# Causal attention beside an FP4 gated layer: one stream over the batches, the layer's products cut up between the score halves

## What is computed

```python
qkv = x @ Wqkv.T                                   # 16 heads of 16 channels
dots = jnp.einsum('bhid,bhjd->bhij', q, k) * scale
dots = jnp.where(causal_mask, -jnp.inf, dots)
attn = jax.nn.softmax(dots, axis=-1)
out = jnp.einsum('bhij,bhjd->bhid', attn, v)
...                                                # heads side by side
return out @ Wout.T + bout

gate = fp4_linear(x, w_gate)                       # 256 -> 704; x and the weights rounded
y = fp4_linear(x, w_up)                            # to FP4 in blocks of 16
h = jax.nn.silu(gate) * y
return fp4_linear(h, w_down)                       # 704 -> 256
```

## Time and profile before

| | us |
|---|---|
| median of 3 runs | 2636.86 (2636.82 to 2639.11) |
| span of the profiled execution | 2634.3 |
| of it from the first scores of `main_phase` on | 1646 |
| TensorE, ScalarE, VectorE busy in the whole span | 2291.5, 1991.2, 1901.9 |

### The profile page before, as it was taken

How to read it: one execution, slowest core, us unless ns; L and a number is a source line. 1 busy time by engine, 2 the same in 40 slices (tenths; PEclk the granted TensorE clock), 3 DMA queues, 4 the chain that set the end, 5 groups by cost and what they waited for, 6 DMA issues and landing times.

```text
span 2634.3 us, 89616 instructions
## 1 busy us (share of the span) xinstructions
PE 2291.5 (87%) x34104; PEld 1276.1 (48%) x34104; DVE 1901.9 (72%) x5676; ACT 1991.2 (76%) x3470; POOL 645.3 (24%) x524
## 2 busy tenths in 40 slices
PE   2896999999999957888888888888888888888888
PEld 1784444444444424444445444545454445444455
DVE  6675999999999965656656666665676565566565
ACT  1343999999999957888875888885888884887885
POOL 3212233333333321212211222211122211222211
PEclk9897999999999989999999999999999999999999
DMA  2576445555555522011012011021111021110101
GB/s 61 177 227 143 69 73 72 73 73 72 73 73 72 73 36 64 21 22 30 23 47 62 18 27 30 16 57 50 24 31 30 15 60 45 27 30 16 27 18 34
DMA packets 94822, 144.19 MB, mean 55 GB/s; under 512 B 25264, under 2 KB 74160, under 8 KB 93872
## 3 DMA queue, kind: packets, MB, share of 16 engines
q1 hardware_dynamic: 73456, 113.77, 23.1%
q10 hardware_dynamic: 16576, 15.73, 1.9%
q0 software_dynamic: 4352, 8.92, 1.4%
HBM read 104.20 MB, written 34.14 MB: 53 GB/s over the span
## 4 chain that ended last, share of the span: by engine, by line
PE 31%; ACT 12%; issue 11%; DVE 7%; ACTq 1%; DMA 0%; SPq 0%; POOL 0%; DVEq 0%; POOLq 0%
ACT probs L1129 10%; PE O L998 8%; PE F L1019 8%; PE F L1059 6%; PE S L977 5%; PE S L1070 2%; PE F L1049 1%; DVE h_norm L1282 1%; DVE o_turned L1344 1%; DVE o_turned L1345 1%; ACT ht_hi L1144 1%; DVE fp_step L1280 1%; DVE fp_step L1278 1%; PE F L1012 1%; PE S L983 0%
## 5 line engine op out<-in xcount | busy, mean ns | idle before, releaser
L1129 ACT ACTIVATE probs<-S 128x1024 f32<-128x1024 f32 (+3 forms) x1280 | 1056.0, 907 | 143.6 <-issue 52.8
L775 ACT ACTIVATE m_excess<-m_DIFF 128x512 f32<-128x512 f32 (+7 forms) x1536 | 646.9, 472 | 85.7 <-PE m_DIFF L735 39.9
L793 DVE CUSTOM_DVE_ANT_0 m_excess<-m_S,m_excess 128x512 f32<-128x512 f32 (+7 forms) x1536 | 700.6, 530 | 11.8 <-PE m_S L735 9.5
L998 PE MATMUL O<-probs,v_sb 64*32 64x512 f32 (+3 forms) x10240 | 611.3, 534 | 33.3 <-DVE o_turned L1345 29.3
L977 PE MATMUL S<-q_st,k_st 64*32 64x512 f16 (+3 forms) x10240 | 432.2, 353 | 180.6 <-ACT probs L1129 140.9
L733 PE MATMUL m_S<-m_k,m_q 128*128 128x512 f16 (+7 forms) x1536 | 482.9, 325 | 26.7 <-DVE m_row_max L793 17.3
L733 PE MATMUL m_DIFF<-m_k,m_q_diff 128*128 128x512 f16 (+7 forms) x1536 | 477.7, 319 | 26.5 <-DMA m_q_diff<-s_q 26.2
L977 PEld LDWEIGHTS S<-q_st,k_st 64*32 64x32 f16 x10240 | 136.1, 90 | 588.7 <-ACT probs L1129 480.4
L677 POOL TENSOR_TENSOR m_q_diff<-m_zero,m_q 48x4096 f16<-48x4096 f16 x32 | 224.4, 7012 | 428.9 <-DMA m_q<-s_q 418.2
L733 PEld LDWEIGHTS m_S<-m_k,m_q 128*128 128x128 f16 x1536 | 148.3, 97 | 275.8 <-DVE m_row_max L793 195.1
L1307 DVE TENSOR_SCALAR tanh<-tanh 128x352 int32<-128x352 int32 x128 | 49.4, 386 | 273.9 <-ACT decay L1139 273.9
(11 more groups left out here) (178 smaller groups left out, 3923.0 us busy)
## 6 DMA issues: line engine op xcount, KB each, us to landing
m_q<-s_q SPq DMA_DIRECT2D x96, 128.0 KB, 3.8
m_k<-s_k SPq DMA_DIRECT2D x96, 128.0 KB, 6.7
m_q_diff<-s_q SPq DMA_DIRECT2D x96, 128.0 KB, 8.0
k_st<-s_k SPq DMA_DIRECT2D x96, 128.0 KB, 4.3
q_st<-s_q SPq DMA_DIRECT2D x384, 32.0 KB
m_k<-s_k SPq DMA_DIRECT2D x96, 124.0 KB, 5.3
a_x<-in_L_attn_x_dram POOLq DMA_DIRECT2D x16, 512.0 KB, 4.8
s_q<-a_part SPq DMA_DIRECT2D x32, 256.0 KB, 2.5
```

Source lines behind the costliest of these rows:

```text
L775: act.activation(excess[u % MAX_EXCESS][:, 0:keys // 2], DIFF[u % MAX_BUFS][:, 0:keys // 2], ACT.Relu) \
L793: dve.tensor_tensor_reduce(larger, S[u % MAX_BUFS][:, 0:keys // 2], larger, 1.0, -3e38, ALU.add, ALU.max, column).then_inc(reduced[u % MAX ...
L998: ins = pe.matmul(O[e][s * SLOT:(s + 1) * SLOT, st.skip:QC], v_sb[st.hg % 2][rows, st.j, s * SLOT:(s + 1) * SLOT], probs[s // 2][st.n % PR ...
L1129: act.activation(probs[half][st.n % PROBS][:, :, 0:st.width], S[half][:, :, 0:st.width], ACT.Exp, scale=scale).then_inc(exped[half], 1)
```

## The change

The four batches become one list of 640 steps, unrolled, with constants in all waits and no loop. The layer's 64 tiles run on through the batches. Each tile has 20 marks, spread evenly over the 10 steps by `place_marks`, which counts a step as its queries plus 110; a mark that falls into the first half of a step is in `early`, the others in `late`. Each engine does its pieces of a mark at the place of `early` or `late` in its own program. On TensorE `early` stands between the two score halves and `late` after the second, ahead of the values. The gate's and the up product are cut into halves of three matmuls, `down` into five pieces of three or four, `h_turn` into two (four and two transposes). The output projection of a batch is made two tiles at a time in `F[0]` and `F[1]` while the next batch's attention runs (from the last three tiles of a batch on, 8 tiles long); only the last ten of the 64 stay for the end. x tiles go into a ring of three of their own, and SyncE issues their loads and the stores. The queries of a chunk are now loaded a chunk ahead. Cut to its core:

```diff
-X_TURN_AT, PAIR_AT, FIRST_PAIR_AT = 2, {4: 0, 7: 1}, {5: 0, 8: 1}
-H_TURN_AT, DOWN_AT = 0, 2
-LAST_H_TURN_AT = 9
+def place_marks(steps, b):
+
+    ends, total = [], 0
+    for st in steps:
+        total += st.width + STEP_COST
+        ends.append(total)
+    at = 0
+    for n in range(TILES):
+        for k in range(MARKS):
+            due = (n * MARKS + k + 0.5) * total / (TILES * MARKS)
+            while ends[at] <= due:
+                at += 1
+            half = ends[at] - (steps[at].width + STEP_COST) / 2
+            (steps[at].early if due < half else steps[at].late).append((b * TILES + n, k))
+
+
+X_TURN_AT = 4
+GATE_AT, UP_AT = ((7, 8), (11, 12)), ((9, 10), (13, 14))
+H_TURN_AT = (16, 17)
+DOWN_AT = (19, 0, 1, 2, 3)
+X_HIGH_AT, GATE_PARTS_AT, H_HIGH_AT = 4, (8, 12), (16, 17)
+X_LOW_AT, SILU_AT, GATED_AT, H_LOW_AT, ADD_DOWN_AT = 5, (9, 13), (10, 14), (17, 18), 4
+X_SCALES_AT, X_ROUND_AT, H_SCALES_AT, H_ROUND_AT = 6, 11, 15, 1
+X_NORM_AT, X_RESCALE_AT, H_NORM_AT, H_RESCALE_AT, BIAS_AT, X_LOAD_AT = 7, 14, 17, 4, 10, 0
+PROJ_FROM, PROJ_TILES = TILES - 3, 8
+PROJ_AT = ((0, 1), (5, 6))
+PROJ_ADD_AT = (2, 7)
+HT_SPLIT = 4
...
+            for st in steps:
+                if st.first:
+                    if st.chunk:
+                        sp.wait_ge(scored[1], last_step[st.chunk - 1] + 1 + PRIMED)
+                    if st.chunk + 1 < chunks:
+                        load_queries(st.chunk + 1)
+                    if st.c == 1 and st.group + 1 < B * NHG:
+                        load_keys(st.group + 1)
+                    if st.hg == NHG - 1 and st.c == 0 and st.b + 1 < B:
+                        load_values(st.b + 1)
+                for t, k in st.early + st.late:
+                    if k == X_LOAD_AT and t + 2 < ALL:
+                        load_tile(t + 2)
+                    if k == X_LOAD_AT and t and projected_at(t - 1, 1) is not None:
+                        store(projected_at(t - 1, 0), 2)
...
+            def gate(t, ch, kk):
+                if kk == 0 and ch == 0:
+                    pe.wait_ge(xt_lo_done, t + 1 + PRIMED)
+                elif kk == 0:
+                    pe.wait_ge(gate_free, 2 * t + 1 + PRIMED)
+                gated_product(0, "gate", ch, kk, gate_ps)
+
+            def up(t, ch, kk):
+                if kk == 0 and ch == 0 and t >= 2:
+                    pe.wait_ge(y_added, t - 1 + PRIMED)
+                    if projected_at(t, 1) is not None:
+                        pe.wait_ge(y_final, projected_at(t, 1) + 1 + PRIMED)
+                elif kk == 0:
+                    pe.wait_ge(gated_done, 2 * t + ch + PRIMED)
+                gated_product(1, "up", ch, kk, up_ps)
...
+                scores(st, 0)
+                for t, k in st.early:
+                    pieces(t, k)
+                scores(st, 1)
+                for t, k in st.late:
+                    pieces(t, k)
+                if st.n:
+                    values(steps[st.n - 1])
...
-                    scores(b, st, 0)
-                    scores(b, st, 1)
-                    if st.n:
-                        values(b, steps[st.n - 1])
-                    if k == DOWN_AT and n >= 2:
-                        down(b, n - 2)
-                    if k == X_TURN_AT:
-                        x_turn(b, n)
-                    if ch is not None:
-                        gate(b, n, ch)
-                        up(b, n, ch)
-                    turned = h_turned_at(n, k, tiles)
-                    if turned is not None:
-                        for part in range(2):
-                            h_turn(b, turned, part)
...
+                exps(st, 0)
+                for t, k in st.early:
+                    pieces(t, k)
+                exps(st, 1)
+                for t, k in st.late:
+                    pieces(t, k)
+            for part in range(2):
+                h_high(ALL - 1, part)
...
+            for st in steps:
+                for t, k in st.early:
+                    pieces(t, k)
+                if st.n and steps[st.n - 1].last:
+                    normalise(steps[st.n - 1].chunk)
+                for t, k in st.late:
+                    pieces(t, k)
+            h_round_(ALL - 1)
```

More of the change, by code:

```diff
@@ L813, in __init__ @@
         self.first, self.last = j == 0, (j + 1) * P == (c + 1) * QC
-        self.chunk = hg * NQC + c
+        self.early, self.late = [], []
+TILES = T // P
+ALL = B * TILES
+MARKS = 20
+STEP_COST = 110
 def attention_steps():
     steps = []
[L819 to L822, removed]
-    return steps
-X_TURN_AT, PAIR_AT, FIRST_PAIR_AT = 2, {4: 0, 7: 1}, {5: 0, 8: 1}
-H_TURN_AT, DOWN_AT = 0, 2
@@ L848, in main_phase @@
 def main_phase(nc, once, loop_sems, wts, ident, exp_scale, x_rows, bout, out_rows, dram):
     steps = attention_steps()
-    nsteps = len(steps)
-    chunks = NHG * NQC
+    chunks = B * NHG * NQC
     last_step = [st.n for st in steps if st.last]
-    tiles = T // P
-    per_tile = nsteps // tiles
-    assert per_tile == 10
     fb = D // QBLK
     hb = I // QBLK
+    inside = sum(projected_at(t, side) is not None for t in range(ALL) for side in range(2))
     primed = []
@@ L966, in _, with scores @@
+            for m in range(projected_at(ALL - 1, 0), ALL, 2):
+                store(m, 2)
+            sp.wait_ge(y_st, 16 * (ALL // 2) + PRIMED)
         @block.tensor
         def _(pe):
[L968 to L973 removed]
+            def scores(st, half):
+                p = st.group % 2
+                pe.wait_ge(exped[half], st.n + PRIMED)
@@ L1030, in up @@
[L1030 to L1047 removed]
+                                    start=kk == 0 and k == 0, stop=kk == KD - 1 and k == len(terms) - 1)
@@ L1067, in project @@
+            values(steps[-1])
+            for piece in range(1, len(DOWN_AT)):
+                down(ALL - 2, piece)
+            for part in range(2):
+                h_turn(ALL - 1, part)
+            for m in range(inside, ALL):
+                if m - inside < SPARE:
+                    pe.wait_ge(exped[m % SPARE // 2], len(steps) + PRIMED)
                 else:
-                    pe.wait_ge(y_final, b * tiles + m - SPARE + 1 + PRIMED)
+                    pe.wait_ge(y_final, m - SPARE + 1 + PRIMED)
@@ new lines, in _ @@
+            dve.wait_ge(norm_ld, 16)
+            x_scales(0)
+            x_round_(0)
+            for st in steps:
+                for t, k in st.early:
[3 more added lines that the diff above has]
+                for t, k in st.late:
+                    pieces(t, k)
+            h_round_(ALL - 1)
+            normalise(chunks - 1)
+            add_down(ALL - 2)
+            for part in range(2):
+                h_low(ALL - 1, part)
```

651 lines of the change are left out of this document (313 added, 338 removed).

## The result

The changed kernel takes 2787.30 us (median of three runs, 2783.93 to 2788.98) where the kernel before takes 2636.86 (2636.82 to 2639.11): 1.056 times the time, 95% interval 1.055 to 1.058. Slower was the right side, but 2662 was forecast and the range ended at 2712. The profiled execution has a span of 2782.2 us, 147.9 more than before; the stage that was summed to 1669 us lasts from 994.4, where the first scores stand, to 2780, so 1786.

The account below looks back on a forecast made before the run. No engine was full: TensorE and ScalarE waited for each other in turn. TensorE's work 1504 + ScalarE's longer steps 40 + VectorE waits 115 + start and tail 10 = 1669 us against 1644, giving 2662 us, range 2575 to 2712.

Parts of the forecast that it names:

- bursts: On TensorE, 987 bursts of layer work instead of 256, at a mean 0.27 us each: 266 us in all.
- the clock: TensorE's granted clock, 1.00 in the steady part; a fall there would make the prediction wrong altogether.
- the waits for VectorE: TensorE waits for work queued behind normalise on VectorE, mostly silu and xt_lo: 115 us, bounds 30 and 170.
- the start: Norms and one tile stand ahead of keys and queries on SyncE's queue: two issues, 1 us at most.
- TensorE's work without bursts: Attention (scores, values, masks) 741 us, plus gated layer and projection 497 us.
- rival B: The burst is free: its weight load runs under the score half, only 0.09 behind it remains; 2538 us, chance 0.08.
- Steps where ScalarE is longer: In steps with no burst or one, ScalarE lasts longer than TensorE: taking the longer step by step adds 40 us.
- Start and tail: After the last step ten projections instead of sixteen, but rounding, normalise and turns in one chain: 10 us, bounds 0 and 20.
- my own case: Slightly slower, 2662 us (2600 to 2710), with waits for VectorE of 60 to 170 us; chance 0.60.
- C: Slower by much: adds, x_turn and silu pile up behind one normalise on VectorE, 190 us of waits; 2737 us, chance 0.10.
- Rival A: The waits for VectorE are covered, as TensorE may reach these gates late anyway: 30 us of waits, 2577 us, chance 0.22.
- The seam: Between batches, about 7 us of TensorE time lost at each of 3 seams goes: a gain of 21, contained in the 337.

Follow-up runs that it names:

- two-part kernel: Changed kernel, small bursts kept, normalise behind the late pieces and cut in two, the rest of it a step later: 2629.8 us, ratio 0.997.
- whole bursts: Changed kernel with layer work in whole groups (gate and up in sixes, h's six transposes together), VectorE's order unchanged: 2673.3 us, ratio 1.013.
- that of 2515 us: Changed kernel with layer work in whole groups (gate and up in sixes) and normalise behind the late pieces in two parts: 2515.4 us, ratio 0.954.
- twelves: Sixes kernel with normalise in two parts, earlier add_down and keys and queries first, but gate and up of a chunk at one mark: 2627.6 us, ratio 0.997.
- the first cut of twelve in the kernel before: Kernel before with six gate products between the score halves and six up products where all twelve stood: 2620.5 us, ratio 0.993.
- the second: Kernel before with three gate products between the score halves, three behind them, six up products behind the values: 2648.3 us, ratio 1.004.

## Why the prediction was wrong, step by step

The forecast was 125 us too low. Four terms of its sum make that up: bursts by 47 us, the clock by 46, the waits for VectorE by 28 and the start by 6; the other terms balance to within some 5 us. The step that failed most is VectorE's order, since the clock's part followed from it: taking that order away gained 157 us.

**TensorE's work without bursts** (741 + 497): held. Scores, values and the products inside a burst have the distances of before (0.16 between products, 0.88 for values with what follows).

**Bursts: 266 forecast, about 313 measured.** The bounds (an entry of 0 to 0.17) held and rival B is out: 0.12 on the way in also behind a score half, as the earlier trace rows had it behind values, and the first weight load does not run under the score half. The earlier trace rows hold no weight loads, so what the prediction says of them there can't be read from them; the rows for it are those at 1503.21 and 1503.32 above. But the mean was mis-sized. 0.27 was taken over from a kernel where every fourth burst holds only transposes; after the change that is 174 of 987, which with my own 0.31 and 0.2 gives 0.29. And the tolls themselves are a little above: 0.32 to 0.34 for products (median of each kind, in the two-part kernel, where little else disturbs them), 0.23 to 0.29 for transposes. Together 47 us too little.

**Steps where ScalarE is longer, 40:** not shown, only not contradicted. 1223 us of work in the stream, 313 of bursts, 143 of waits for VectorE, 46 of clock and 17 of tail make 1742 of 1786; 44 are left, and no experiment took this term alone.

**VectorE's order: waits of 115 forecast, 143 measured.** This is the step that failed, and in its parts more than in its sum. On silu and xt_lo I put 103, chunk end by chunk end; TensorE waits 39 for them (26.9 and 11.8), and 68 in the kernel without projections, where nothing else makes it late. On the adds in projection tiles I put 12, bounds 0 and 35; TensorE waits 82 for adds, the three larger rows `<- DVE y` of the list after. The prediction had the mechanism in one sentence ("`up` or `x_turn` waits for them behind normalise") and worked it out nowhere, while it worked out four gates to a tenth of a us. F[0] and F[1] have two users more in those tiles, the projections, each released by an add in the same queue, and each add is needed by TensorE within one or two marks. So the sum came within 28 us by luck: one part was 64 too high, the other 70 too low, and the rest, 22, is ht_lo, o_turned and the tail.

**The clock: 0 forecast, some 46 us by estimate.** The trace of before showed 1.00 in the steady part, and the prediction treated that as a property of the stage and not of the waits in it, though it named a fall as the sign of being wrong altogether. The change filled TensorE's many short waits and put few long ones in their place. Nearly all the pieces at 1.2 GHz stand by waits of 2.2 to 3.7 us, and most of these are for the adds. In the kernel that differs only by the place of normalise they are nearly gone: 106 us in the changed kernel and with whole bursts, 42 with normalise last, 11 with it in two parts. The 157 us of that comparison hold the clock too, so they are not to be added to it.

**Start and tail: 10 forecast.** The start costs 6.5 and not the 1 I had for SyncE's queue: I counted the issues that moved and overlooked the wait that moved with the keys. The tail, from the last value product to 2780, is 17 us of work and waits, of which 15 were in the 497.

**Rivals.** By its waits the result lies in my own case: 143 us of its 60 to 170, and C was to decide from 175 on. Only waits and clock together, 189, reach C's 190. The bursts' 47 and the start's 6 on top lift C's 2737 to 2790, by 2787 measured. C had a chance of 0.10 and the range left it out. Its mechanism, adds, x_turn and silu behind one normalise, is there in the adds above all; that they push the next tile's work into the next chunk's end was not shown, and the clock was in no rival's sum. So C's near hit is partly luck. Rival A, with the waits covered, was built on purpose: 32 us of waits remain in the two-part kernel, near A's own 30, and it runs in 2630, not 2577; the 53 between are, to within a few us, the bursts and the start.

**The seam** is gone, as said: in the kernels with one stream there is no gap in the exponentials at a change of batch; behind the start ScalarE's longest wait for scores or their mask is 4.9 us in the changed kernel and 3.6 in that of 2515 us, where a seam had 17.6. What that is worth in time was not tried alone.

## What to carry to other kernels

When work of two kinds shares one engine's queue, list for each buffer of the busiest engine who must empty it, and what stands in front of that instruction in its queue, in every kind of tile, the rare ones too: a long block that itself waits for the busiest engine, as normalise does, must not stand in front of a short one it waits for. Cut such a block where it frees its buffer, and let the rest run a step later. Choose the size of a burst from both sides: small enough that the other engine gets its next input in time, and no smaller, since each costs a toll; here sixes are over 100 us faster than threes and than twelves, though with the twelves the place of the up products changed too.

## What the runs showed of the hardware

- TensorE's granted clock fell to 1.2 GHz in 23 pieces of 3.4 or 6.8 us in a stage that was otherwise 90% busy: 106 us in all, by estimate 46 of them lost. 22 stand by single waits of 2.2 to 3.7 us and one by a wait of 1.7, but four waits of 2.9 or 3.0 us had none. A wait of 2.90 us was followed by half a projection in 1.15 us in place of 0.52 and values on 512 columns in 1.71 in place of 0.85 to 0.88.
- Going from products in 64x32 tiles to 128x128 ones and back costs 0.12 us in, 0.10 on the first product and 0.09 out, whether a score half or values stand ahead; the Trainium skill, "TensorEngine Tiling (Array Packing)", Key Properties, has a change of tiling mode drain the engine, which fits, without a figure for it.
- A burst's toll of 0.31 us does not always show in the time: the first cut of twelve in the kernel before gave 17 us, the second took 28.
